# The value half of the up-projection read by VectorE straight from PSUM

## What is computed

```python
x = x + attention(layernorm(x), ctx, Wq, Wk, Wv, Wfc, bfc)        # 32 heads of 16, 8 groups
h = layernorm(x).astype(fp8)
ff_gate = h @ w_gating[0].astype(fp8)                             # 512 -> 2048
ff1     = h @ w_gating[1].astype(fp8)                             # 512 -> 2048
activations = gelu(ff_gate) * ff1
out = x + activations.astype(fp8) @ w_linear.astype(fp8)          # 2048 -> 512
```

## Time and profile before

| | |
|---|---|
| median of 3 runs | 465.05 us (464.51 to 467.0) |
| profiled execution, its own time | 464.56 us |
| profiled execution, span from first to last instruction | 462.4 us |
| granted TensorE clock, mean | 0.985 |
| busy: TensorE / VectorE / ScalarE / GpSimd | 427.8 / 334.4 / 313.2 / 236.4 us |
| copies of the value half (L866) | 64, 37.5 us |
| products (L1149) | 64, 31.8 us |
| exponentials (L840 and L843) | 256, 154.8 us |

### The profile page before, as it was taken

How to read it: one execution, slowest core, us unless ns; L and a number is a source line. 1 busy time by engine, 2 the same in 40 slices (tenths; PEclk the granted TensorE clock), 3 DMA queues, 4 the chain that set the end, 5 groups by cost and what they waited for, 6 DMA issues and landing times.

```text
span 462.4 us, 11802 instructions
## 1 busy us (share of the span) xinstructions
PE 427.8 (93%) x4620; PEld 344.4 (74%) x4620; DVE 334.4 (72%) x704; ACT 313.2 (68%) x578; POOL 236.4 (51%) x226
## 2 busy tenths in 40 slices
PE   7857969889999999999999999999999999899997
PEld 6736848767787878877787877877787878558973
DVE  4776587976897579966897678975897678565542
ACT  6848784987379745977369745887469744895541
POOL 5577982696228813684228813685228712392000
PEclk9997798999999999999999999999999999999999
DMA  8897669264602560035501551035501351000001
GB/s 281 293 261 282 223 180 292 85 207 128 170 3 54 155 137 28 1 89 155 125 4 46 158 121 48 1 91 148 132 3 38 81 115 48 2 25 24 3 26 45
DMA packets 21240, 49.79 MB, mean 108 GB/s; under 512 B 4673, under 2 KB 5185, under 8 KB 21185
## 3 DMA queue, kind: packets, MB, share of 16 engines
q1 hardware_dynamic: 20862, 48.24, 36.3%
q10 hardware_dynamic: 322, 0.80, 0.6%
HBM read 23.86 MB, written 4.19 MB: 61 GB/s over the span
## 4 chain that ended last, share of the span: by engine, by line
PE 61%; DVE 11%; POOL 10%; issue 8%; ACT 7%; DMA 2%; ACTq 1%; POOLq 0%; SPq 0%; DVEq 0%
PE bank L647 16%; PE bank L667 9%; POOL plo L1300 7%; PE bank L446 6%; PE bank L448 6%; PE bank L447 6%; PE bank L554 5%; PE bank L521 4%; DVE mneg L1084 4%; PE bank L481 3%; PE bank L572 2%; PE bank L574 2%; ACT phi L843 1%; DMA qs<-cq 1%; DVE prod L1149 1%
## 5 line engine op out<-in xcount | busy, mean ns | idle before, releaser
L1300 POOL TENSOR_TENSOR plo<-p,phi 128x512 f16<-128x512 f32 x128 | 149.8, 1182 | 59.8 <-ACT phi L843 58.9
L647 PE MATMUL bank<-x2T,wgate 128*128 128x128 fp8e4 x2048 | 131.4, 221 | 3.6 <-DVE xr L1162 3.2
L647 PEld LDWEIGHTS bank<-x2T,wgate 128*128 128x128 fp8e4 x2048 | 117.0, 99 | 19.2 <-issue 12.3
L1084 DVE TENSOR_REDUCE mneg<-bank 128x4 fp32r<-128x512 f32 x128 | 84.5, 685 | 7.7 <-PE bank L521 7.3
L840 ACT ACTIVATE p<-bank 128x512 f32<-128x512 f32 x128 | 77.5, 606 | 18.3 <-PE bank L554 17.6
L843 ACT ACTIVATE phi<-bank 128x512 f16<-128x512 f32 x128 | 77.3, 604 | 0.0
L667 PE MATMUL bank<-wlin,act 128*128 128x512 fp8e4 x256 | 72.0, 378 | 0.0
L862 ACT ACTIVATE gate<-bank 128x512 bf16<-128x512 f32 x64 | 38.2, 597 | 49.8 <-PE bank L647 37.0
L866 ACT CAST ff<-bank 128x512 bf16<-128x512 f32 x64 | 37.5, 587 | 49.3 <-PE bank L647 49.3
L521 PE MATMUL bank<-kmask,cq 128*128 128x512 f32 x128 | 57.5, 474 | 4.7 <-DVE mneg L1084 2.8
L554 PE MATMUL bank<-qs,ks 98*128 98x512 f32 x128 | 55.2, 431 | 6.7 <-DMA qs<-cq 2.8
(11 more groups left out here) (117 smaller groups left out, 810.1 us busy)
## 6 DMA issues: line engine op xcount, KB each, us to landing
qs<-cq SPq DMA_DIRECT2D x90, 128.0 KB, 2.5
stage<-in_w SPq DMA_DIRECT2D x14, 512.0 KB, 5.2
ks<-khl SPq DMA_DIRECT2D x96, 64.0 KB, 2.0
cin<-in_ctx SPq DMA_DIRECT2D x8, 512.0 KB, 4.2
xr<-in_x SPq DMA_DIRECT2D x16, 256.0 KB, 4.3
out<-xr SPq DMA_DIRECT2D x16, 256.0 KB, 2.7
xr<-in_w SPq DMA_DIRECT2D x6, 512.0 KB, 6.0
raw_g<-in_w SPq DMA_DIRECT2D x4, 512.0 KB, 5.8
```

The costliest lines, as they stand in the source:

```text
L647: mm = pe.matmul(out[:, h * SEQ:(h + 1) * SEQ], wgate8[:, UH * v + h, kk, part, :], x2T[:, b % NB, kk, :], start=kk == 0, stop=kk == KT - 1)
L1084: dve.tensor_reduce(dst[:, :, 2 * half:2 * half + 2, j].rearrange("p a r -> p r a"), bank_of("S", q, i, s)[:, :].rearrange("p (r a k) -> p ...
L1300: pool.tensor_tensor(plo[:, e % PBUF, :], p32[:, e % P32BUF, :], phi[:, e % PBUF, :], ALU.subtract).then_inc(plo_ok, 1)
```

## The change

The bf16 tile `ff` and ScalarE's copy into it go, and with them the semaphore `ff_ok`. VectorE's product takes its second operand from the PSUM bank of the value half, as float32, and waits for TensorE's `ff_done` in place of the copy. All four places at which TensorE waited for `ff_ok` before it wrote into such a bank now wait for `prod_ok`, the end of the product. The order of the instructions that remain is the same on every engine.

```diff
-        ff = sb("ff", [P, 2, UH * SEQ], BF16)
...
 # weigh_values (TensorE), first two tiles of a round
                         pe.wait_ge(gelu_ok, units_through(p - 1))
-                        pe.wait_ge(ff_ok, units_through(p - 1))
+                        pe.wait_ge(prod_ok, units_through(p - 1))
...
 # turn_out (TensorE)
                 elif b:
-                    pe.wait_ge(ff_ok, units_through(p) - 1)
+                    pe.wait_ge(prod_ok, units_through(p) - 1)
...
 # up (TensorE)
                 if k >= 2:
-                    pe.wait_ge(ff_ok if part else gelu_ok, u - 1)
+                    pe.wait_ge(prod_ok if part else gelu_ok, u - 1)
...
-            def ff_out(u):
-                act.wait_ge(ff_done, u + 1)
-                act.copy(ff[:, u % 2, :], up_bank[u % 2][1][:, :]).then_inc(ff_ok, 1)
...
                     gate_out(u)
                     if p and k == 3:
                         x2_out(c_b)
-                    ff_out(u)
...
             def product(u):
                 dve.wait_ge(gelu_ok, u + 1)
-                dve.wait_ge(ff_ok, u + 1)
-                dve.tensor_tensor(prod[:, u % 2, :], gate[:, u % 2, :], ff[:, u % 2, :], ALU.mult).then_inc(prod_ok, 1)
+                dve.wait_ge(ff_done, u + 1)
+                dve.tensor_tensor(prod[:, u % 2, :], gate[:, u % 2, :], up_bank[u % 2][1][:, :], ALU.mult).then_inc(prod_ok, 1)
```

More of the change, by code:

```diff
@@ L239, in xattn_ffn_kernel @@
             sem("x2T_done"), sem("x2T_ok"))
-        gate_done, ff_done, ff_ok, gelu_ok, prod_ok, act_ok = (
-            sem("gate_done"), sem("ff_done"), sem("ff_ok"), sem("gelu_ok"), sem("prod_ok"), sem("act_ok"))
+        gate_done, ff_done, gelu_ok, prod_ok, act_ok = (
+            sem("gate_done"), sem("ff_done"), sem("gelu_ok"), sem("prod_ok"), sem("act_ok"))
         lin_done, out_ok = sem("lin_done"), sem("out_ok")
```

## The result

The changed kernel takes 465.95 us (median of 20 runs, 464.99 to 468.5), the kernel before 464.56 us (20 runs). The ratio is 1.0038, with a 95% interval from 1.0021 to 1.0056: slower by 0.4% (1.8 us), where I forecast 0.3% faster. The profiled execution took 465.79 us, with a span of 463.7.

A forecast was written before the change was run, and what follows sets the result against it. The prediction took TensorE as the bound (61% of the chain). Its terms, -1.2 + 0.75 - 1.15 - 0.25 + 0.27 = -1.58 us, against the runs' median of 465.05 us gave 463.5 us, range 461.3 to 466.4 us.

The forecast's parts named there:

- the forecast's estimate: Middle blocks: VectorE needs 2.27 us of TensorE's 2.39 us per unit, leaving 0.12 us to spare instead of 0.39.

The follow-up runs named there:

- e8: Kernel before up to and with round 5, the changed form in rounds 6 and 7 alone; ratio 0.9959, median 462.64 us.
- e7: Changed kernel with the old form in round 0 and, in rounds 1 to 5, ScalarE's idle copy of a constant tile; ratio 0.9945, median 462.61 us.
- e11: Changed kernel with the old form in round 0 and, in rounds 1 to 5, ScalarE's context copies and table load placed by semaphores; ratio 1.0001 to the kernel before.
- e2: Kernel before, copy and SBUF product kept, with only TensorE's four waits moved from the copy to the product; ratio 1.0032 to the kernel before.
- e1: Changed kernel with ScalarE copying a constant SBUF tile, which nobody reads, in place of the removed copy; ratio 1.0009 to the kernel before.

## What to carry to other kernels

Work taken off an engine that is not the bound still moves that engine's later work forward; follow it to the next engine and ask which instructions it will now run beside. Here 1.2 us of freed ScalarE put GpSimd's context subtractions and its first low part on VectorE's clamps, at a time when, by the forecast's estimate, the longer product had taken most of VectorE's slack. The same change pays where nothing follows (rounds 6 and 7), so it is worth applying by stage. e8 does only that and is 0.41% faster than the kernel before; e7, with the change in rounds 1 to 5 as well and an idle copy to hold ScalarE, is 0.55% faster, which the noise doesn't tell from e8. In rounds 1 to 5 it gains 0.35 us in all.

## What the runs showed of the hardware

VectorE's bf16 to fp8 clamp of 128x512 takes 0.43 us, and up to 1.34 us when a GpSimd subtraction of 1.16 us begins 0.10 us before it (401.35 and 401.45): it ends 0.28 us behind GpSimd's end, and GpSimd is not slowed (1.16 us there, 1.17 the median of all 128). A float32 PSUM operand makes the bf16 product 0.26 us longer and takes it out of this contention. In e11, ScalarE's table load did not wait for the semaphore on which the activation behind it waits (187.86 against 188.82). And TensorE's granted clock fell to its 1.2 GHz level in e2's trace (0.54 over 3.5 us), behind waits of 1.14 and 0.45 us, and not in the traces of the kernel before and of e1, which have the same waits; it cost 1.1 us, as much as the whole of most terms here.
